# A tuned fp32 transformer block on one core: the mixer's softmax in three tiles of 128 rows a group, in place of four tiles of 96, with its own order of the steps

## What is computed

```python
h = tok(x)                      # 64 patch tokens of 192: ffn, windowed attention, ffn
h = concatenate([h, txt], 1)    # 96 tokens a sample
h = h + attn(_layernorm(h))     # the mixer: gated conv, attention with 12 heads of 16, ffn
h = h + ffn(_layernorm(h))      # attention with 12 heads of 64, gated by experts

def _attn(x, qkv_w, qkv_b, num_heads):          # in the mixer, N = 96, hd = 16
    q, k, v = ...(x @ qkv_w + qkv_b)
    scores = jnp.einsum('bqhd,bkhd->bhqk', q, k) * scale
    attn = jax.nn.softmax(scores, axis=-1)
    out = jnp.einsum('bhqk,bkhd->bqhd', attn, v)
```

## Time and profile before

| what | us |
|---|---|
| runs, median of 3 | 595.31 |
| lowest and highest | 593.17, 597.15 |
| the profiled execution | 590.72 |
| its span, first to last instruction | 588.9 |
| PE busy in the span | 525.0 |
| DVE busy | 418.2 |
| ACT busy | 311.8 |
| POOL busy | 98.4 |

### The profile page before, as it was taken

One profiled execution on the slowest core, in us unless ns is written; L12 is line 12 of the kernel. 1 busy time (PEld: TensorE's weight loads), 2 busy tenths in 40 slices (PEclk: granted clock), 3 DMA queues, 4 the chain that ended last, 5 costly groups with the idle time before them and its releaser, 6 DMA issues.

```text
span 588.9 us, 10749 instructions
## 1 busy us (share of the span) xinstructions
PE 525.0 (89%) x4337; PEld 400.0 (68%) x4337; DVE 418.2 (71%) x910; ACT 311.8 (53%) x520; POOL 98.4 (17%) x85
## 2 busy tenths in 40 slices
PE   4899889778978999999998999999968999899696
PEld 4766567556766676778786666877846677686474
DVE  4145767699568767687868677687828888857982
ACT  0234444555335555767636555866535649544762
POOL 7032400000310224200010124100000022011200
PEclk9799999999999999999999999999997999999999
DMA  9993020000000000100000000000000000000000
GB/s 217 298 209 112 1 61 1 7 2 1 1 0 2 1 2 1 55 8 2 1 21 2 2 1 1 1 1 2 1 21 1 1 2 1 1 1 21 2 1 22
DMA packets 12674, 15.99 MB, mean 27 GB/s; under 512 B 6235, under 2 KB 10048, under 8 KB 12240
## 3 DMA queue, kind: packets, MB, share of 16 engines
q1 hardware_dynamic: 9712, 12.71, 8.7%
q10 hardware_dynamic: 2400, 2.00, 1.1%
q0 software_dynamic: 512, 0.59, 0.5%
HBM read 14.11 MB, written 1.18 MB: 26 GB/s over the span
## 4 chain that ended last, share of the span: by engine, by line
PE 68%; DVE 16%; ACT 8%; POOL 3%; issue 2%; SPq 1%; DMA 1%; ACTq 0%; DVEq 0%; POOLq 0%
PE ps L686 15%; PE ps L999 8%; PE ps L696 8%; PE ps L676 7%; DVE smax L1683 4%; PE ps L1057 4%; PE ps L819 4%; PE ps L1189 3%; PE ps L1169 2%; PE ps L879 2%; PE ps L777 2%; DVE psum L1697 2%; POOL side_wide L1928 2%; PE ps L1145 2%; PE ps L1047 2%
## 5 line engine op out<-in xcount | busy, mean ns | idle before, releaser
L1683 DVE TENSOR_REDUCE smax<-ps 96x12 f32<-96x1152 f32 x32 | 43.2, 1349 | 25.8 <-PE ps L1047 19.9
L1354 ACT ACTIVATE pr<-ps,less 96x96 f32<-96x96 f32 x112 | 28.6, 334 | 25.9 <-DVE less L1685 25.9
L1364 ACT ACTIVATE pT<-ps 96x1152 f32<-96x1152 f32 x28 | 31.5, 1126 | 15.0 <-PE ps L1057 15.0
L1697 DVE TENSOR_REDUCE psum<-pr 96x12 f32<-96x1152 f32 x28 | 37.5, 1339 | 2.0 <-ACT pr L1359 1.9
L1057 PE MATMUL ps<-w_ident,pr 96*96 96x96 f32 x336 | 33.3, 249 | 3.0 <-DVE pr L1709 2.1
L1057 PEld LDWEIGHTS ps<-w_ident,pr 96*96 96x96 f32 x336 | 28.2, 127 | 8.1 <-DVE pr L1709 4.0
L1391 ACT ACTIVATE squares<-ps 128x1536 f32<-128x1536 f32 x12 | 17.4, 1451 | 29.3 <-PE ps L696 23.4
L1928 POOL TENSOR_TENSOR side_wide<-attn,w_mask 128x1024 f32<-128x1024 f32 (+1 forms) x12 | 22.2, 1868 | 58.1 <-ACT attn L1248 52.2
L1047 PE MATMUL ps<-b_kB,heads 32*96 32x192 f32 x192 | 20.2, 376 | 11.9 <-ACT b_kB L1334 6.7
L1796 DVE TENSOR_REDUCE ss<-squares 128x24 f32<-128x1536 f32 x12 | 21.0, 1749 | 11.2 <-ACT squares L1391 11.2
L676 PE MATMUL ps<-w_cqkv,side_c 64*96 64x384 f32 (+1 forms) x96 | 27.4, 500 | 0.0
(11 more groups left out here) (357 smaller groups left out, 1322.9 us busy)
## 6 DMA issues: line engine op xcount, KB each, us to landing
x_in<-in_xT SPq DMA_DIRECT2D x3, 768.0 KB, 4.4
b_kB<-in_cqkv SPq DMA_DIRECT2D x1, 1152.0 KB
w_cqkv<-in_cqkv SPq DMA_DIRECT2D x1, 864.0 KB
out<-side_c ACTq DMA_DIRECT2D x3, 288.0 KB, 2.5
w_cqkv<-in_cqkv SPq DMA_DIRECT2D x1, 855.0 KB
...
```

Source lines behind the costliest of these rows:

```text
L1354: m = act.activation(w.y.pr[:, s % 2, h * N:(h + 1) * N], t[0:N, h // 4, h % 4 * N:(h % 4 + 1) * N], ACT.Exp, scale=head ** -0.5, bias=les ...
L1364: act.activation(w.y.pT[:, :, :].rearrange("p (b h) t -> p b (h t)", b=3), t[0:N, :, 0:4 * N], ACT.Copy)\
L1683: dve.tensor_reduce(mx, t, AX.X, ALU.max).then_inc(w.S[stage + "_sub"], 1)
L1697: dve.tensor_reduce(psum[:, s % 2, :], e, AX.X, ALU.add).then_inc(w.S[done], 1)
```

## The change

Scores, softmax and transposes of the mixer no longer go by sample. Tile `s`, of three, holds 32 queries of each of the four samples: rows 0 to 31 are queries 32s to 32s+31 of sample 0, rows 32 to 63 those of sample 1, and so on: 128 rows. Each pair is now four products of 32x32 stationary and 32x192 moving, one for each sample, into four strips of 32 rows of the result. DVE and ACT do the same operations as before on 128 rows, three times a group. A turned tile is twelve transposes of 128 rows to 96x128, and ACT copies 96x1536 to `b_pT`, a view of the memory of `side_q` and `side_k` (now one tensor, `side_qk`), which the `c` chain uses for its q and k at other times. It is laid out by head, sample and query, so that a sample's 96 queries stand together; hence every `b_o` needs all three turned tiles.

```diff
-        pr = sb("pr", [N, 2, NH * N])
+        pr_all = sb("pr", [128, 2, NH * N])
+        pr = pr_all[0:N]
...
+        b_pT = side_qk[:, :].rearrange("p (h s t) -> p h s t", h=NH, s=GS)
...
             def b_s(w, s):
...
-                    m = pe.matmul(t[0:N, bank, second * 2 * N:(second + 1) * 2 * N],
-                                  b_qT[r, c, s * N:(s + 1) * N], b_kBv[r, :, c, s * N:(s + 1) * N], start=True, stop=True)
+                    for of in range(GS):
+                        at = of * N + s * 32
+                        m = pe.matmul(t[32 * of:32 * of + 32, bank, second * 2 * N:(second + 1) * 2 * N],
+                                      b_qT[r, c, at:at + 32], b_kBv[r, :, c, of * N:(of + 1) * N], start=True, stop=True)
...
-                turn_p(w, ("b_pt", s), s)
+                t = slot(w, ("b_pt", s))
+                for h in range(NH):
+                    m = pe.transpose(t[0:N, h // 4, h % 4 * 128:(h % 4 + 1) * 128], pr_all[:, s % 2, h * N:(h + 1) * N],
+                                     w_ident[:, :])
+                m.then_inc(fill_sem(w, ("b_pt", s)), 1)
 
             def b_o(w, s):
-                for sem_read, value in reads_before(w, ("b_o", s), ("b_pT", s + 1), ("b_vB", 1)):
-                    pe.wait_ge(sem_read, value)
-                if w.first:
-                    pe.wait_ge(s_pad, 4)
+                for sem_read, value in reads_before(w, ("b_o", s), ("b_pT", 3), ("b_vB", 1)):
+                    pe.wait_ge(sem_read, value)
...
-                    m = pe.matmul(t[row:row + 2 * HD, c * N:(c + 1) * N], b_vB_all[:, s, h, :], pT_all[:, at, :],
+                    m = pe.matmul(t[row:row + 2 * HD, c * N:(c + 1) * N], b_vB_all[:, s, h, :], b_pT[:, at, s, :],
...
+            def b_pt(w, s):
+                act.wait_ge(fill_sem(w, ("b_pt", s)), fill_count(w, ("b_pt", s)))
+                t = slot(w, ("b_pt", s))[0:N]
+                act.activation(b_pT[0:N, :, :, s * 32:(s + 1) * 32],
+                               t.rearrange("p b (h s q) -> p (b h) s q", s=GS, q=32), ACT.Copy).then_inc(w.S["b_pT"], 1)
...
         def _(dve):
+            dve.memset(side_k[N:128, :], 0.0).then_inc(s_set, 1)
+            dve.wait_ge(s_set, 1)
...
-            pool.wait_ge(s_pad, 3)
-            pool.memset(pT_all[N:128, :, :], 0.0).then_inc(s_pad, 1)
...
-                elif w.c > 0:
+                elif w.c == 0:
+
+                    pool.memset(pT_all[N:128, :, :], 0.0).then_inc(s_pad, 1)
+                    pool.wait_ge(s_pad, 4)
+                else:
```

The table is written anew. Two pieces of it, for group 0, before and after:

```diff
-    b_e.1:0 b_n.0:0 b_n.1:0 a_in.0:1 b_pt.0:0 b_s.2:0=2 b_e.2:0 b_o.0:0=1 b_pt.1:0 b_e.3:0 a_cv.0:1 a_cv.1:1
+    b_e.1:0 b_n.0:0 b_n.1:0 a_pb a_in.0:1=1 b_pt.0:0=2 b_s.2:0 b_e.2:0 b_n.2:0 b_pt.1:0 a_in.1:1 b_pt.2:0=0
```

More of the change, by code:

```diff
@@ L96 @@
-    c_pt.2:1 c_v.3:1=1 c_n.3:1 a_cv.0:3 a_cv.1:3 c_pr.0:1=4 c_o.2:1=0 a_gt.0:3 c_pt.3:1=5 a_cv.2:3 a_gt.1:3
-    c_pr.1:1=0 c_o.3:1=6 a_gt.2:3 a_out.0:3=5 a_out.1:3 a_out.2:3=5 c_pr.2:1=5 b_u.1:3 b_qk:3 b_s.0:3=1 b_s.1:3
-    b_n.0:3 b_e.0:3 e_u:2=0 b_e.1:3 b_n.1:3 b_v:3 b_pt.0:3=5 b_s.2:3=2 b_o.0:3=0 b_pt.1:3 warm.3 b_s.3:3=5 b_e.2:3
-    b_n.2:3 b_e.3:3 b_n.3:3 b_o.1:3=0 e_qk.0:2 b_pt.2:3=5 e_v.0:2 b_o.2:3=2 b_pt.3:3 b_pr.0:3=6 b_pr.1:3 b_o.3:3=5
-    b_pr.2:3 e_qt.0:2=2 e_g:2 e_v.1:2 b_u.2:3=3 e_qk.1:2=0 e_qk.2:2 b_f1.0:3 b_f1.1:3 e_qt.1:2 e_s.0:2 e_s.1:2=0
@@ new lines @@
+    d_out.1:0=0 d_out.2:0=3 a_f2.1:1=7 a_h2.1:1=4 b_u.1:0=5 a_ht:1 b_qk:0 a_u:1=6 b_v:0 b_e.0:0 b_s.0:0 b_s.1:0
+    b_e.1:0 b_n.0:0 b_n.1:0 a_pb a_in.0:1=1 b_pt.0:0=2 b_s.2:0 b_e.2:0 b_n.2:0 b_pt.1:0 a_in.1:1 b_pt.2:0=0
+    b_o.0:0=7 b_o.1:0=0 b_o.2:0=6 b_o.3:0=2 a_cv.0:1 a_cv.1:1 a_cv.2:1 b_pr.0:0=5 warm.2 a_gt.0:1 a_gt.1:1 a_gt.2:1
+    b_pr.1:0=4 b_pr.2:0=3 a_em:2=1 a_out.0:1=7 b_u.2:0 a_out.1:1=4 a_out.2:1=7 a_en:2 b_f1.0:0=2 b_f1.1:0 b_u.1:1=0
+    b_f2.0:0 b_f2.1:0=3 a_wc.3 b_f2.2:0=4 b_qk:1=5 b_v:1=2 c_u:0 a_x0:2 b_s.0:1 b_e.0:1 b_n.0:1 a_f1.0:2=0 b_s.1:1
@@ new lines @@
+    c_o.0:0 c_pt.1:0=5 c_s.2:0=2 c_s.3:0 c_e.2:0 c_e.3:0 c_v.2:0 c_n.2:0 a_in.0:2=2 a_in.1:2=5 c_o.1:0=3 c_v.3:0=0
+    c_n.3:0 c_pt.2:0=5 a_cv.0:2 a_cv.1:2 c_pr.0:0=2 c_o.2:0=5 c_pt.3:0=1 a_gt.0:2 a_cv.2:2 a_gt.1:2 c_pr.1:0=0
+    c_o.3:0=1 a_gt.2:2 a_out.0:2=4 a_out.1:2=5 a_out.2:2=7 c_pr.2:0=5 c_u:1=2 b_u.1:2 c_g:1=5 b_qk:2=2 a_en:3
+    a_em:3=6 b_s.0:2 b_v:2=5 a_x0:3=3 b_e.0:2 b_s.1:2=4 b_e.1:2 warm.3=7 b_n.0:2 b_n.1:2 a_f1.0:3 a_f2.0:3=4
+    a_h2.0:3 b_pt.0:2=0 b_s.2:2=5 b_e.2:2 a_qk:3=0 b_n.2:2 b_pt.1:2=4 a_v:3 b_pt.2:2 a_s.0:3 b_o.0:2=2 b_o.1:2=1
@@ new lines @@
+    a_gt.1:3 b_f2.2:2 c_o.2:1=0 c_pt.3:1=4 c_pr.1:1 c_o.3:1 a_gt.2:3 a_out.0:3=7 a_out.1:3=0 a_out.2:3=4 c_pr.2:1=6
+    b_u.1:3=4 b_qk:3 e_u:2=5 b_s.0:3 b_s.1:3=3 b_n.0:3 b_e.0:3 b_e.1:3 b_v:3=6 e_v.0:2 b_n.1:3 b_pt.0:3=4 b_s.2:3=0
+    b_e.2:3 b_n.2:3 e_qk.0:2 b_pt.1:3 b_pt.2:3=5 b_o.0:3 b_o.1:3=7 b_o.2:3=1 b_o.3:3=3 b_pr.0:3=7 b_pr.1:3 b_pr.2:3
+    e_v.1:2=1 e_g:2 e_qt.0:2 b_u.2:3=6 e_qk.1:2 e_qk.2:2=0 b_f1.0:3=3 b_f1.1:3 e_qt.1:2=4 e_s.0:2 e_s.1:2 b_f2.0:3
+    e_n.0:2 e_e.0:2 e_e.1:2 e_n.1:2 e_qt.2:2=0 b_f2.1:3=7 e_pt.0:2=3 e_s.2:2 e_o.0:2=3 e_pt.1:2=5 e_e.2:2 e_v.2:2=3
```

120 lines of the change are left out of this document (58 added, 62 removed).

## The result

| what | before | after |
|---|---|---|
| runs, median | 594.24 us (4 runs, 591.83 to 597.15) | 571.17 us (4 runs, 570.54 to 571.50) |
| span of the profiled execution | 588.9 us | 569.3 us |
| PE busy, and the rest of the span | 525.0, 63.9 | 513.4, 55.9 |
| mean granted clock of PE | 0.980 | 0.988 |

The ratio is 0.961 (95% interval 0.956 to 0.966): 3.9% faster, 23.1 us by the medians, 19.6 us by the profiled executions. I had forecast 584.8, a gain of 10.5 us, and a range from 575.0. The direction was right; the gain I forecast was less than half of the measured one by the medians.

The account below looks back on a forecast made before the run. PE was taken to set most of the time (68% of the last chain), DVE some. Terms -7.5 - 2.0 - 1.5 - 3.0 + 2.5 + 1.0 = -10.5 us, set against the 595.3 us median, gave 584.8 us; range 575 to 597.

Parts of the forecast that it names:

- Group 0, walked, and `a_em` in it: Group 0's attention: u's turns begin 3.5 us earlier and a_em's 4.06 us fill PE's wait, together 7.5 us gained.
- `a_em` as a step by itself: Group 2's a_em runs on PE while DVE and POOL make group 0's u, so its 4.06 us needn't be done later.
- The gates: Group 0's c_g, 5.7 us of DVE steps, moved inside group 1's softmax: costs 0 to 5.7 us, taken as +2.5.
- The clock: PE's array at its lower level in parts of groups 0 and 3; no main-sum term, 2.4 us either way kept at the start.
- PE's own work: Turns and score products on PE: 1.0 us saved in each group, with no saving for the values.
- Idle time in groups 1 to 3: PE's waits shrink by 1.0 us in group 1, 0.5 in group 2, and 0.7 plus 1.3 in group 3.
- Late values in groups 1 to 3: Values stand behind the last copy, where PE or ACT may wait: between 0 and 4.4 us, taken as +1.0.
- Start: Program start: DVE's new memset, at most 2.7 us, hides in a 5.93 us DMA wait; moving POOL's memset costs nothing.
- One of the signs I had named: The forecast would be wrong if PE's group period, one a_em to the next, didn't shorten.
- PE takes it back: Rival: PE is full in groups 1 and 2, so only its own 4.0 us saving stays, 591.3 us; chance 0.23.
- Strips don't overlap: Rival: a score tile takes up to 4.5 us, about 617 us, or 596 at half overlap; chance 0.12 for both.
- DVE's relief counts in full: Rival, the large gain: groups 1 to 3 give up most idle time, clock stays up, 7 us more, 578; chance 0.15.

Follow-up runs that it names:

- e3: Changed kernel with a_em, a_en and a_x0 of group 2 put back where the kernel before had them, around group 1's first scores: 580.40 us, +9.2.
- e15: Kernel before, four tiles, with a_em of group 2 moved behind b_pr of group 0 and a_en behind a_out.1: 602.50 against 595.36 us, ratio 1.012.
- e4: Changed kernel with c_u and b_u.1 of group 1 back ahead of b_qk and b_v, so nothing covers the wait for u: 584.93 us, +13.8.
- e5b: Changed kernel with group 0's gates c_g back ahead of group 1's softmax, all PSUM banks but c_g's own kept: 582.31 us, +11.1.
- e17: Kernel before, four tiles, with the changed kernel's moves between group 0's b_pr and group 1's first scores, and gates inside group 1's softmax: 594.82 against 595.19 us, ratio 1.001.
- e16: Kernel before, four tiles, with the changed kernel's moves between group 0's b_pr and group 1's first scores, gates still ahead of the softmax: 597.63 us, ratio 1.004.
- e10: Changed kernel with every mixer score product issued twice, 96 records a tile in place of 48: 591.96 us, +20.8.
- e6b: Changed kernel with the order and PSUM banks of the kernel before up to the first scores of group 0: 575.57 us, +4.4.
- e8: Changed kernel with four unread DVE reductions (5.4 us) ahead of the third tile's maximum in each group: 597.63 us, 26.5 us above the changed kernel.
- e12: Kernel before with the fourth sample's DVE softmax work cut to one head of twelve, order kept: 595.35 against 593.46 us, ratio 1.004.
- e1: Three tiles of 128 rows with the order of the kernel before, b_o behind the third turn: 633.15 against 595.49 us, ratio 1.061.
- e2: Four tiles of 96 rows with the changed kernel's order, not every buffer handed on in time: 623.53 us, ratio 1.048.
- e9b: Changed kernel with four more unread warm products in bank 7 ahead of group 3's first scores, other banks kept: 572.39 us against 571.2.
- e14: Changed kernel with a score tile's 24 products in another order, pairs 0, 1, 2 taking turns inside each sample: 571.76 us, tile 1.21 us.

## Why the prediction was wrong

The steps that failed are two terms that the sum put at nothing and one that had the wrong sign: the wait for `u` in front of `c_u`, in a stretch that I never read (5.3 us of idle time, now 0.5); the clock (10 us less at the lower level, up to 5 us of PE's time); and the gates, +2.5 us forecast, where group 1 with the gates in it became 2.5 us shorter and their old place costs 11.1 us in the new order. I had PE at about 520 us of work and it came to 513.4; I had about 5.5 us less idle time and it was 8.0. Term by term:

- **Group 0, walked, and `a_em` in it (-7.5).** The number is nearly right. The turns of `u` begin 32.4 us behind the first scores where it was 35.2, 2.8 us sooner, with the 4.06 us of `a_em` already done: 6.9 us. The picture behind it is not: I had PE's idle time there shrinking from 10 us to 3. From the first scores to `u` it is 6.4 us before and 6.6 after. The wait for the keys went (2.64 to 0.62 us), and PE's other work in the stretch got shorter; before, 6.8 us of it ran at the lower level, now none.
- **`a_em` as a step by itself (-4.06 of these).** I priced a moved step by its own length. In the new order putting it back costs 9.2 us (e3), since it is also the head of the chain `a_em`, `a_en`, `a_x0`; alone, in the kernel before, the move loses 7 us (e15). So neither number is the price of the step: it depends on what stands around it.
- **A row I did not look at (0).** Of PE's waits I read the attention stretches only. The stretch behind, 145.7 to 180.5, had 5.3 us of idle time, 3.4 of them one wait for `u` in front of `c_u`. The new table puts `b_qk` and `b_v` there; e4 gives all of it back and more, 13.8 us (with six banks shifted).
- **The gates (+2.5).** Wrong in sign. From the first scores of group 1 to those of group 2 it is 2.5 us shorter, though 1.6 us of the gates' products came in. In the new order their old place costs 11.1 us (e5b); in the old order the new place is no loss either (e17 594.82 us, e16 597.63).
- **The clock (0).** I had put it in the rival of the large gain only. At the lower level PE spent 2 x 0.020 x 588.9 = 24 us before and 2 x 0.012 x 569.3 = 14 us now, 10 us less, at most 5 us of PE's time. The medians differ by 3.5 us more than the profiles, and the clock fits that too: the profiled execution of before was a lucky one, with 0.980 where the median of its runs is 0.971.
- **PE's own work (-3.0 in groups 1 to 3, 4.0 with group 0).** Against before it is 12 x 1.21 - 16 x 1.13 = -3.6 for the scores (I took 1.35 a tile, -1.8), 12 x 1.44 - 16 x 1.12 = -0.6 for the turns (I took 1.31, and 1.44 is above my upper bound; -2.2) and 4 x (2.82 - 4 x 0.82) = -1.8 for the values, to which I gave no saving: together -6.0. That it is near is partly luck, as the errors in scores and turns cancel. e10 shows that PE's time counts in full in the new order.
- **Idle time in groups 1 to 3 (-1.0, -0.5, -2.0).** From the first scores of group 1 to the end it fell by 1.7 us.
- **Late values in groups 1 to 3 (+1.0).** PE waits 1.5 us for the last copy in group 3 and nothing in groups 1 and 2. In group 0 it waits 1.5 us too.
- **Start (0).** 1.5 us earlier in the trace; with what hangs on it, 4.4 us (e6b).

One of the signs I had named was useless: from one `a_em` to the next it is 132.6 us before and 151.2 now, because `a_em` of group 2 itself moved.

Of the rivals, "PE takes it back" falls by e10 and e8. "Strips don't overlap" falls by the trace: 48 records in 1.21 us. By the 62 ns a MATMUL that the Trainium skill ("TensorE: Matmul & The Clock Gate", section "Wait — 56ns, not 53.3ns?") gives for hardware decode off, it would have been 3.0 us. The trace has starts 6.7 ns apart, so that bound does not hold here; which way the chip decoded, no run here shows. "DVE's relief counts in full" came nearest with 578, but not by its own sum: it had groups 1 to 3 give up most of their idle time, which fell by 1.7 us there, and the clock still falls once in group 3. What holds of it is that in the new order DVE's time counts in full (e8: 26.5 us for 20.7 us of DVE), and in the old one not at all (e12: nothing). That is behind the failed steps: I priced the relief in the waits of the order of before, and the change had an order of its own, made so that the relief could be used. Neither e1, e2, e12, e15, e16 nor e17 gains anything; all parts together give 23 us.

What stays open: how much of the losses of e1 to e4 is the order and how much the banks; the new order of groups 1 to 3, of which no part was taken back by itself; what the clock is worth apart from the waits it comes with; and the price of the late values, which can't be undone in this layout and was not tried. No version was found that beats the changed kernel; e9b and e14 equal it.
